# Cross-attention set-up merged with its batch loop; x in four pieces, query weights by column block, 257th values ahead of the queries

## The reference, cut to what matters

```python
# x: (32, 32, 512), ctx_1024: (32, 257, 512), H = 16 heads, D_K = 32
def proj(x, W, b):
    return (x @ W.T + b).reshape(B, -1, H, D_K).transpose(0, 2, 1, 3)
Q = proj(query, Wq, bq)            # query = _layernorm(x)
K = proj(key, Wk, bk)              # key = value = ctx_1024
V = proj(value, Wv, bv)
scores = jnp.einsum('bhqd,bhkd->bhqk', Q, K) / jnp.sqrt(jnp.float32(D_K))
thr = _softplus_t(raw_thresholds)[None]
scores = jnp.where(scores <= thr, NEG, scores)
attn = jax.nn.softmax(scores, axis=-1)
x = jnp.einsum('bhqk,bhkd->bhqd', attn, V)
return x.transpose(0, 2, 1, 3).reshape(B, S, H * D_K) @ Wo.T + bo
...
x = x + _L0_xattn_ref(_layernorm(x, axis=-1), ctx_1024, ctx_1024, ...)
```

## Time and profile before

| | |
|---|---|
| time, median of 3 runs | 1808.55 us |
| lowest and highest run | 1808.08 and 1811.35 us |
| the profiled execution: its own time | 1806.73 us |
| the profiled execution: its span | 1804.9 us |
| TensorE busy | 1677.1 us, 93% of the span |
| VectorE, ScalarE, GpSimd busy | 61%, 47%, 26% |
| mean granted TensorE clock | 0.962 of full speed |

### The profile page before, as it was taken

One profiled execution on the slowest core, in us unless ns is written; L12 is line 12 of the kernel. 1 busy time (PEld: TensorE's weight loads), 2 busy tenths in 40 slices (PEclk: granted clock), 3 DMA queues, 4 the chain that ended last, 5 costly groups with the idle time before them and its releaser, 6 DMA issues. The chain is left out here.

```text
span 1804.9 us, 26236 instructions
## 1 busy us (share of the span) xinstructions
PE 1677.1 (93%) x9152; PEld 1438.6 (80%) x9152; DVE 1099.8 (61%) x2213; ACT 854.8 (47%) x1192; POOL 466.4 (26%) x340
## 2 busy tenths in 40 slices
PE   5999999999998599989998999799975999999997
PEld 4899999999998388768886887687864888888886
DVE  5445555555554666653336666634337999999995
ACT  3444444444343423253334222533324788888884
POOL 0344444443443244300002443300001121212121
PEclk9899999999999799989999999799986999999999
DMA  4111011001100410013324000132323234545622
GB/s 162 48 36 36 24 35 35 30 28 35 35 24 0 141 48 0 1 59 98 99 71 159 24 0 1 59 95 92 126 99 126 83 116 163 174 163 179 254 73 64
DMA packets 35215, 139.61 MB, mean 77 GB/s; under 512 B 4753, under 2 KB 5393, under 8 KB 28433
## 3 DMA queue, kind: packets, MB, share of 16 engines
q1 hardware_dynamic: 29984, 126.75, 19.8%
q0 software_dynamic: 5168, 12.06, 3.4%
HBM read 227.92 MB, written 12.85 MB: 133 GB/s over the span
## 5 line engine op out<-in xcount | busy, mean ns | idle before, releaser
L1730 DVE TENSOR_TENSOR e_w<-e_raw,e_w 128x2048 fp32r<-128x2048 f32 x138 | 311.2, 2283 | 14.7 <-ACT e_w L1591 14.7
L1591 ACT ACTIVATE e_w<-e_raw 128x2048 fp32r<-128x2048 f32 x138 | 264.0, 1917 | 46.4 <-DMA e_raw<-in_we 21.2
L80 PE MATMUL bank<-e_w,e_xT 128*128 128x512 f32 x1104 | 273.8, 397 | 1.4 <-DVE e_xT L1748 1.4
L80 PEld LDWEIGHTS bank<-e_w,e_xT 128*128 128x128 f32 x1104 | 206.1, 190 | 43.5 <-DVE e_xT L1748 1.8
L80 PE MATMUL bank<-ctx,wk 128*128 128x258 f32 x1536 | 195.3, 287 | 3.5 <-PEq L195 3.5
L1324 PE MATMUL bank<-fw,hh 128*128 128x512 f32 x768 | 189.0, 396 | 9.9 <-DVE hh L1182 9.9
L80 PE MATMUL bank<-x2T,fw 128*128 128x512 f32 x768 | 189.3, 396 | 6.3 <-DVE fw L1133 6.3
L80 PEld LDWEIGHTS bank<-ctx,wk 128*128 128x128 f32 x1536 | 189.5, 192 | 3.6 <-issue 3.6
L80 PE MATMUL bank<-wv,ctx 128*128 128x512 f32 x768 | 189.2, 395 | 0.0
L1324 PEld LDWEIGHTS bank<-fw,hh 128*128 128x128 f32 x768 | 146.3, 191 | 42.1 <-issue 10.5
L80 PEld LDWEIGHTS bank<-x2T,fw 128*128 128x128 f32 x768 | 146.5, 192 | 37.6 <-issue 6.7
(11 more groups left out here) (238 smaller groups left out, 2725.9 us busy)
## 6 DMA issues: line engine op xcount, KB each, us to landing
e_raw<-in_we SPq DMA_DIRECT2D x143, 1024.0 KB
fraw<-in_wf SPq DMA_DIRECT2D x64, 512.0 KB, 3.4
ctxraw<-in_ctx SPq DMA_DIRECT2D x32, 514.0 KB, 3.3
wraw<-in_wa SPq DMA_DIRECT2D x20, 512.0 KB, 5.0
X<-in_x SPq DMA_DIRECT2D x2, 1024.0 KB, 6.7
acc_d<-X SPq DMA_DIRECT2D x8, 256.0 KB, 9.1
xh_d<-A SPq DMA_DIRECT2D x8, 256.0 KB, 8.5
out<-acc_d SPq DMA_DIRECT2D x4, 512.0 KB, 5.8
```

Source lines behind the costliest of these rows:

```text
L80: last = nc.tensor.matmul(out, lhs(t, a), rhs(t, b), start=start and n == 0, stop=n == len(steps) - 1)
L1591: nc.scalar.activation(w[pos][:, 0, :, :], raw[pos][:, :, :], ACT.Copy).then_inc(m["w_hi"], 1)
L1730: nc.vector.tensor_tensor(w[pos][:, 1, :, :], raw[pos][:, :, :], r(w[pos][:, 0, :, :]), ALU.subtract).then_inc(m["w_lo"], 1)
```

## The change

The two blocks become one. Each engine's list now has the set-up's instructions followed by the loop's, with semaphores in place of the meeting between them.

- x arrives in four pieces of two tiles. The first two stand at the head of SP's list; the last two stand behind Wq, vec, ctx_last and Wv.
- The statistics are taken in three groups: tiles 0 and 1, tiles 2 and 3, and, after Wq has been split, tiles 4 to 7.
- Wq is split in four column blocks of 128x512 on ScalarE and VectorE, between the work on the turned tiles; query group n waits for block n alone.
- The turned tiles go to four banks in place of two.
- The 257th values stand before q(0) in TensorE's list, behind the turns of tiles 0 to 3. They wait for Wv to land.
- The small instructions for the threshold stand early, before the second half of the statistics; the last two stand behind the split of Wo.
- The context of batch 0 is split between the turned tiles 5 and 6 (ScalarE), and its low part is made by GpSimd then.
- Wo is split on ScalarE between `query_hi(5)` and `query_hi(6)`; on VectorE it stays behind `query_lo(7)`.
- TensorE, before the first key product, waits for `w_lo` to reach `DC + 3`, that is for the low parts of Wq (4), Wv, Wk and Wo.
- Buffers of both parts are placed together; those of the loop that are not needed in the set-up lie over `xT` and `wq`.

```diff
-                    for i in range(2):
-                        tiles = range(4 * i, 4 * i + 4)
-                        dve.wait_ge(x_in[i], 16)
...
-                    weight_lo(0)
-                    turned_lo(2)
...
+                    xv = a["x"].rearrange("(t p) d -> p t d", p=P)
+                    for i in range(2):
+                        sp.dma_start(X[:, 2 * i:2 * i + 2, :], xv[:, 2 * i:2 * i + 2, :]).then_inc(x_in[i], 16)
+                    sp.dma_start(ident[:, :], a["ident"]).then_inc(id_in, 16)
+                    for i in range(2):
+                        sp.dma_start(raw[i][:, :, :], weights[i][0]).then_inc(w_in[i], 16)
+                        if i == 0:
+                            sp.dma_start(vec[:, :], a["vec"]).then_inc(vec_in, 16)
+                            sp.dma_start(craw[:, :, :], a["ctx_last"]).then_inc(cl_in, 16)
+                    for i in range(2, 4):
+                        sp.dma_start(X[:, 2 * i:2 * i + 2, :], xv[:, 2 * i:2 * i + 2, :]).then_inc(x_in[i], 16)
+                    sp.dma_start(raw[2][:, :, :], weights[2][0]).then_inc(w_in[2], 16)
+                    sp.dma_start(ctxraw[0][:, :, :], a["ctx"][0].rearrange("p (c n) -> p c n", c=DC)).then_inc(ctx_in[0], 16)
+                    sp.wait_ge(w_hi, DC)
+                    sp.wait_ge(w_lo, DC)
+                    sp.dma_start(raw[0][:, :, :], weights[3][0]).then_inc(w_in[3], 16)
...
 @block.gpsimd
+                            else:
+                                pool.wait_ge(vec_in, 16)
+                                pool.wait_ge(q_lo, 2 * DC)
                             spread_q(b)
...
+                    context_lo(0, 0, 0)
+                    pool.wait_ge(misc_in, 48)
                     body(0, True, False)
...
 @block.scalar
+                    query_weight_hi(0)
+                    turned_hi(0)
+                    query_weight_hi(1)
+                    turned_hi(1)
+                    turned_hi(2)
+                    query_weight_hi(2)
+                    turned_hi(3)
+                    query_weight_hi(3)
+                    act.wait_ge(th_dve, 1)
+                    nc.scalar.activation(th[:, 2, :], th[:, 0, :], ACT.Exp, scale=-1.0).then_inc(th_act, 1)
+                    act.wait_ge(th_act, 1)
+                    nc.scalar.activation(th[:, 3, :], th[:, 2, :], ACT.Ln, bias=1.0).then_inc(th_act, 1)
+                    act.wait_ge(vl_ps, 1)
+                    nc.scalar.activation(vlast[:, :, :], bank[4][:, 0:DC * NB].rearrange("p (c n) -> p c n", c=DC), ACT.Copy).then_inc(vl_ok, 1)
+                    act.wait_ge(vec_in, 16)
+                    for n in range(4):
+                        query_hi(n)
+                        turned_hi(4 + n)
+                        if n == 1:
+                            act.wait_ge(ctx_in[0], 16)
+                            nc.scalar.activation(ctx[0][:, 0, :, 0:SK], ctxraw[0][:, :, :], ACT.Copy).then_inc(ctx_hi, 1)
+                    weight_hi(1)
+                    query_hi(4)
+                    weight_hi(2)
+                    query_hi(5)
+                    weight_hi(3)
+                    query_hi(6)
+                    query_hi(7)
...
 @block.vector
+                    statistics_of(range(0, 2))
+                    statistics_of(range(2, 4))
+                    normalise_x(0)
+                    normalise_x(1)
+                    normalise_x(2)
+                    query_weight_lo(0)
+                    normalise_x(3)
+                    turned_lo(0)
+                    query_weight_lo(1)
+                    turned_lo(1)
+                    turned_lo(2)
+                    turned_lo(3)
+                    query_weight_lo(2)
...
+                    query_weight_lo(3)
+                    statistics_of(range(4, 8))
+                    for n in range(4):
+                        normalise_x(4 + n)
+                        query_lo(n)
+                        turned_lo(4 + n)
+                    weight_lo(1)
+                    query_lo(4)
+                    query_lo(5)
+                    weight_lo(2)
+                    query_lo(6)
+                    query_lo(7)
+                    weight_lo(3)
...
 @block.tensor
+                    for t in range(4):
+                        turn_x(t)
+                    pe.wait_ge(w_in[1], 16)
+                    pe.wait_ge(cl_in, 16)
+                    for dc in range(DC):
+                        for c in range(DC):
+                            last = nc.tensor.matmul(bank[4][:, dc * NB:(dc + 1) * NB], raw[1][:, c, dc * P:(dc + 1) * P], craw[:, c, :],
+                                                    start=c == 0, stop=c == DC - 1)
+                    last.then_inc(vl_ps, 1)
+                    pe.wait_ge(xT_lo, 4)
+                    for n in range(4):
+                        query(n)
+                        turn_x(4 + n)
+                    pe.wait_ge(xT_lo, NT)
+                    for n in range(4, 8):
+                        query(n)
+                    pe.wait_ge(vl_ok, 1)
+                    pe.wait_ge(w_lo, DC + 3)
+                    pe.wait_ge(misc_in, 48)
```

More of the change, by code:

```diff
@@ L166, in cross_attention @@
         same_head = sb("same_head", [P, P])
[L167 to L170, removed]
+        ctxraw = [sb(f"ctxraw{i}", [P, DC, SK]) for i in range(2)]
+        ctx = [sb(f"ctx{i}", [P, 2, DC, SKE], F32R) for i in range(2)]
+        qbd = sb("qbd", [P, 2, DC, P], F32R)
+        raw = [sb(f"raw{i}", [P, DC, D]) for i in range(3)]
+        craw = sb("craw", [P, DC, NB])
+        stats = sb("stats", [P, NT, 6])
+        mv = sb("mv", [P, NT, 2])
+        veps = sb("veps", [P, NT])
+        rstd = sb("rstd", [P, NT])
+        xh = sb("xh", [P, 2, D])
+        th = sb("th", [P, 5, DC])
         with ExitStack() as inner:
@@ L371, in cross_attention @@
[L371 to L392 removed]
+            T_BANK = (0, 1, 5, 6)
@@ L420, in _ @@
                 def _(pool):
-                    nc.gpsimd.memset(r(ctx[1][:, :, :, SK:SKE]), 0.0).then_inc(zeroed, 1)
+                    nc.gpsimd.memset(mhalf[:, :], -0.5).then_inc(half_set, 1)
+                    for i in range(2):
+                        nc.gpsimd.memset(r(ctx[i][:, :, :, SK:SKE]), 0.0).then_inc(zeroed, 1)
+                    pool.wait_ge(half_set, 1)
+                    for i in range(3):
+                        pool.wait_ge(veps_ok, i + 1)
+                        cols = slice(2 * i, 2 * i + 2) if i < 2 else slice(4, 8)
+                        nc.gpsimd.tensor_tensor(rstd[:, cols], veps[:, cols], mhalf[:, 0:cols.stop - cols.start], ALU.pow).then_inc(rstd_ok, 1)
                     def context_lo(it, k, b):
@@ new lines, in turned_hi, with query_hi @@
+                    def turned_hi(t):
+                        act.wait_ge(x_turned, t + 1)
+                        nc.scalar.activation(xT[:, 0, :, t * P:(t + 1) * P], bank[T_BANK[t % 4]][:, :].rearrange("p (c n) -> p c n", c=DC),
+                                             ACT.Copy).then_inc(xT_hi, 1)
+                    def query_hi(n):
+                        half, dc = n // 4, n % 4
+                        act.wait_ge(q_ps, n + 1)
+                        nc.scalar.activation(qT[:, 0, dc, half * 512:(half + 1) * 512], bank[2 + n % 2][:, :], ACT.Identity,
+                                             bias=col("bq", dc)).then_inc(q_hi, 1)
@@ L518, in _, with statistics_of @@
                 def _(dve):
+                    def statistics_of(tiles):
+                        for t in tiles:
+                            dve.wait_ge(x_in[t // 2], 16)
+                            nc.vector.bn_stats(stats[:, t, :], X[:, t, :]).then_inc(x_stats, 1)
+                        for t in tiles:
+                            dve.wait_ge(x_stats, t + 1)
+                            nc.vector.bn_aggr(mv[:, t, :], stats[:, t, :]).then_inc(x_aggr, 1)
+                        dve.wait_ge(x_aggr, tiles.stop)
+                        nc.vector.tensor_scalar(veps[:, tiles.start:tiles.stop], mv[:, tiles.start:tiles.stop, 1], 1e-5, None, ALU.add).then_inc(veps_ok, 1)
@@ L622, in _, with turn_x, query @@
                 def _(pe):
+                    pe.wait_ge(id_in, 16)
+                    def turn_x(t):
+                        pe.wait_ge(xh_ok, t + 1)
+                        if t >= 4:
+                            pe.wait_ge(xT_hi, t - 3)
+                            pe.wait_ge(xT_lo, t - 3)
+                        for c in range(DC):
+                            last = nc.tensor.transpose(bank[T_BANK[t % 4]][:, c * P:(c + 1) * P], xh[:, t % 2, c * P:(c + 1) * P], ident[:, :])
+                        last.then_inc(x_turned, 1)
+                    def query(n):
+                        half, dc = n // 4, n % 4
+                        if n >= 2:
+                            pe.wait_ge(q_lo, n - 1)
+                        if n < DC:
+                            pe.wait_ge(w_lo, n + 1)
```

(7 more changed lines are left out.)

257 lines of the change are left out of this document (68 added, 189 removed).

## The result

The changed kernel took 1800.74 us (median of 4 runs, 1798.10 to 1802.95) against 1809.27 before (1808.08 to 1811.35): ratio 0.9948, interval 0.9936 to 0.9961. 8.5 us won, where 5.2 were forecast and 1803.3 us predicted. The profiled execution's span is 1796.3 us, 8.6 less than 1804.9.

What follows compares the result with a forecast made beforehand. TensorE, busy 93% of the span and never idle in the loop, was taken as the bound, so the first key product's start decides. Gains of 1.3 + 3.6 + 0.3 = 5.2 us gave 1803.3 us, range 1799.5 to 1807.5.

Steps and rivals of the forecast that it cites:

- Head: Set-up until q(0): with x in pieces and the 257th values in front, q(0) starts at 19.8, not 21.11; 1.3 us won.
- the first rival: 257th values in the head cost the same at low clock as at high: 7.2 us won, 1801.3 us; chance 0.12.
- price of 6.9 us: The 32 instructions of the 257th values, ahead of q(0), take 0.215 us each at low clock, 6.9 us.
- bounds for the values: Limits on the 257th values' time ahead of q(0): 4.06 us as measured before, 8.0 us at 0.25 each.
- Middle: From q(0) through the query groups: q(1) to q(4) keep 11.55 us, the next four 11.18; nothing gained or lost.
- End of the set-up: Behind q(7): values, table load, threshold and meeting leave the path; keys start at 52.2, not 55.75; 3.6 us won.
- VectorE's term: VectorE's last split, of Wo, behind q(7): keeps its 2.29 us beside GpSimd's spread_q(0); 4.2 if VectorE paid.
- Clock at the keys: First keys after the idle time behind q(7): 0.3 us won, bounds 0.5 lost and 2.7 won.
- The loop neither gives nor takes: Batch loop: instructions kept and TensorE never idle, so gains before its first key product arrive whole; 0 us.
- the tenth of a us per batch: Batch loop: a pace change of this size would show the prediction wrong.
- Slower, for lack of Wv: Head: 257th values wait for a late Wv; at half transfer rate 2.2 us are lost, 1810.8 us; chance 0.04.
- the third rival: Head gives nothing back: 2.6 to 2.9 us remain, or 1.7 if VectorE pays for GpSimd; 1805.7 to 1806.9; chance 0.25.

Runs made afterwards that it cites:

- a_again: The changed kernel measured once more, with nothing altered: 1801.64 us, 0.9943 of the kernel before.
- b_again: The kernel before the change measured once more, with nothing altered: one run of 1809.68 us.
- old_tail: Changed kernel with Wo's high part behind query_hi(7), the threshold behind it and awaited before the keys, values still in front: 1805.08 us, 0.9975.
- no_wo_wait: Changed kernel whose first keys no longer wait for Wo's low part; that wait stands ahead of Wo's first use: 1797.72 us, 0.9925.
- thr_early: As no_wo_wait, with the threshold's last two small instructions ahead of VectorE's split of Wv: 1799.23 us, 0.9931 of the kernel before.

## Why the prediction was right, point by point

Sign and range were right; the size was short by 3.3 us of 8.5. By the last softmax of the loop, each of the two profiles of before against each of the two of the changed kernel, the gain is 8.3, 6.4, 8.7 and 6.7 us, so between 1.2 and 3.5 more than forecast. What is said below of the head and of the clock at the keys depends on which two profiles are taken.

- **Head, 1.3 us.** In the profile above it was 2.9: the values took 4.61 and not 6.9, as in the first rival, at a clock that was high when they began, behind nothing but turns, and that fell inside them; q(0) then took 5.36 for 4.32, which I had left unchanged. In a_again, with the values at 6.88, it was 0.9 (q(4) at 36.25), and that this is near 1.3 is luck: q(0) started 2.3 us earlier than before and not 1.3 (the turns started at 8.4, not 9.0, and Wv was there), and then took 5.47, 1.15 more. All seven profiles with the values whole and in front have 4.98 to 5.47 for q(0), so this term was wrong. Against b_again, where the kernel before also took 5.46, the head gains 4.0 and 2.0. The price of 6.9 us held in six of the seven. The mis-sized term is the head, by a clock that differs between executions of either kernel; the bounds for the values (4.06 and 8.0) held.
- **Middle, nothing.** Right: 11.59 and 11.54 us from q(1) to q(4) for 11.55, then 11.18 and 11.20; ScalarE's context split was hidden; tile 4 was ready in time.
- **End of the set-up, 3.6 us.** Right: 3.59; the remaining idle time, forecast 3.9 and released by Wo's low part, was 3.81. old_tail undoes it, no_wo_wait removes what is left. That VectorE's term stands beside GpSimd was right here (2.28), because VectorE had started first; it was wrong as a rule. In old_tail GpSimd started first and the same split took 3.17, and a short VectorE instruction behind it paid in the changed kernel (1.85), two in no_wo_wait. In the changed kernel that one was off the path, since the keys waited for Wo.
- **Clock at the keys, 0.3 us.** Fell again, as forecast, and came back earlier: 7.53 for 8.60, so 1.07, within the bounds. Against b_again, where the keys took 7.78, it is 0.25, the 0.3 that was forecast: the 1.07 is as much the first profile of before as the change.
- **The loop neither gives nor takes.** Wrong by 0.77 us: its instructions stayed, its buffers moved. It is under the tenth of a us per batch that the prediction gave as a sign of being wrong.
- **Sum.** 2.9 + 3.59 + 1.07 + 0.77 = 8.3, the 8.34 of the last softmax. With a_again's head, 0.9 + 3.59 + 1.10 + 0.77 = 6.4. The medians' 8.5 and 9.3 us have the unequal rests of the span in them; how much of them is scatter stays open.
- **Slower, for lack of Wv.** Wv landed at 12.7; TensorE waited 0.15 us for it.
- **Slips in the prediction's own sums.** With GpSimd's cost put on VectorE, the third rival leaves 2.9 - 1.9 = 1.0 us and not 1.7, which is 1807.6 us, just outside the stated range. The gain that a late Wv would eat is 5.2, not 4.9, so it is gone at 18.1 and not 17.9. Neither moves the forecast.

## What to carry to other kernels

Work moved out of a tail into a hole is worth only what no other wait of the same tail covers: here the wait for Wo, which the keys did not read, hid the whole move, and narrowing that wait was worth 3.0 us. When a wait is removed, read next what stands in the other engines' lists behind it, short instructions too, and which of two engines starts first. Judge steps of some us by the start of the same instruction in two profiles, and take the clock at the head from more than one execution.

## What the runs showed of the hardware that was not expected

- A VectorE instruction of 4 elements beside a GpSimd elementwise one took 1.85 or 2.11 us in place of 0.16, and ended within 0.03 us of GpSimd's. With VectorE's 2.28 us instruction first, GpSimd's took 3.78 in place of 1.89; with GpSimd's first (old_tail), it took 1.89 and VectorE's 3.17. In each of these pairs the second to start paid, whatever its length. It is no rule for every pair: VectorE's low parts of the keys, with one input in PSUM, took 0.44 us each beside GpSimd in thr_early.
- Where a TensorE operand starts mattered: the first context buffer, which every second batch reads, moved by 32 bytes cost the loop 0.90 us over 31 batches (one run). By the sizes of the buffers ahead of it, it then starts 32 bytes off a multiple of 64, as in the kernel before, whose loop took 0.77 us longer than the changed one's.
- The view of the granted clock lists 1.00 from the start also where it is low: in a_again no change is listed before 51 us, yet the values' 32 instructions took 6.88 us, with weight loads of 333 ns for 192. What follows here for the head rests on durations.
